# Layer-norm scaling moved from ScalarE to VectorE, and transposes moved behind attention

## The chip, the cores and the metric

The kernel runs on all 8 NeuronCores of one Trainium2 chip. Each core works on 4 of the 32 sequences and the cores don't talk to each other. The metric is the device time of the slowest core, in microseconds (us).

## The reference

For x of 32 sequences x 2048 tokens x 1024, the layer computes

```python
xn = _layernorm(x, axis=-1)
x = x + attn(xn, w_in, w_out) + ffn(xn, weight_q, weight_scale, bias)
```

Here attn is sliding-window attention with 16 heads of 64 and blocks of 512 tokens: each block of queries sees its own block of keys and the one before, masked to a window of 512, with a bias per head that grows with distance, a softmax and an output projection. The ffn quantises xn per token to 8 bits (scale = max|xn|/127, rounded), multiplies by an int8 weight matrix and scales back.

## The kernel before

A tile is one block of 512 tokens; a core has 16 of them, four per sequence. The first block of a sequence (n=0: tiles 0, 4, 8, 12) has 4 chunks of keys per head, the others (n>0) have 8. The program is written out by hand: each engine gets its list of instructions in the order in which the Python code emits them, and semaphores alone tie the engines together. The order of emission is the order of execution on each engine, and the DMAs of SP's queue stand in one such list too.

`emit_pre(t)` loads x of a tile into `x_tm` and computes its statistics on DVE (VectorE): bn_stats, bn_aggr, a maximum and a minimum over each token, and then a chain of small instructions for 1/sqrt(var) and the scales. The last of them is L351, and L354 is an empty instruction that raises the semaphore V. `emit_xnq_compute(t)` writes xn = x*rstd + bias in bf16 into `xn4`, with four ACT (ScalarE) instructions of 128x1024 (L366). `emit_xnq_transpose(t)` quantises x on DVE (`xq_chain`: two instructions into PSUM, L387 and L391, and two roundings, L396 and L400, for each of the four groups of 128 tokens), transposes xn and xq on PE (TensorE) by multiplying with the identity (L418), and copies the results from PSUM with ACT (L426). `emit_qkv(t)` computes q, k (L461, copies L472) and v (L484, copies L493), with the weights of q and k streamed by SP.

`emit_attn(t)` goes through 8 groups of two heads. For each chunk of keys PE computes scores (L632), ACT takes the exponential into one of 8 slots of `pe_buf` (L653, cut into slices of 64 to 512 columns by head), DVE multiplies a 128x128 part by a triangular mask (L666), and PE multiplies by V (L610), three chunks behind the scores. The two output banks of a group are normalised during the next group: ACT takes log and exp of the sum (L534, L538), PE spreads it over 64 partitions (L552, "ones"), ACT copies it (L557), and DVE multiplies (L563 into `o_fm`, L571 into `o_stage`, which a DMA brings to the upper half of `o_fm`). `emit_proj(t)` then does the output projection (L705) and the ffn's matmul (L717), and DVE adds up bias, x and both results (L729 to L744) and SP stores them.

PSUM has 8 banks, handed out in turn by `Banks`. In attention two of them hold outputs and six circulate.

In the main loop the statistics of tile t+1 and its L366 stand ahead of the attention of tile t on DVE and ACT; the quantising and the transposes of tile t+1 are called from a hook after group 4 of the attention of tile t.

Of the kernel before, what the change touches and what calls it, by code (L numbers as in the profile page):

```python
# [11 lines left out]
ALU = mybir.AluOpType  # L12
AF = mybir.ActivationFunctionType
# [128 lines left out]
def build_nc(n_seq=4, n_blk=4, taps=None):  # L142
    taps = taps or {}
    nc = bass.Bass("TRN2", target_bir_lowering=False)
    NT = n_seq * n_blk
# [19 lines left out]
    with ExitStack() as ctx:  # L165
# [13 lines left out]
        xn4 = sb("xn4", [128, 4096], BF16)  # L179
# [14 lines left out]
        stt = sb("stt", [128, 64], F32)  # L194
# [3 lines left out]
        C_MV, C_XMAX, C_XMIN, C_VEPS, C_SQ, C_R0, C_RTMP, C_RSTD = 0, 8, 12, 16, 20, 24, 28, 32  # L198
        C_BIASA, C_MX, C_AMAX, C_AM2, C_INV, C_ALPHA, C_BETA = 36, 40, 44, 48, 52, 56, 60
# [5 lines left out]
        P = Prog(sem_names)  # L205
# [7 lines left out]
        for dst, src in [(wsb_sb[:, :], wsbh), (biasb_sb[:, :], biasbh), (ident_sb[:, :], identh),  # L213
# [4 lines left out]
                  waits=[("LG", lg0)])  # L218
        lg0 = dma("gpsimd", wq_sb[:, :], wqh.rearrange("p a b -> p (a b)"), "LG",
                  waits=[("LG", lg0)])  # L220
# [15 lines left out]
        xn4_free = []  # L236
# [7 lines left out]
        zb_free = [[], []]  # L244
        zln_free = [[], []]
        prevT = 0
        stt_S_readers = 0
        TS = {}

        def tapit(name, src_ap, waits, engq="sync"):  # L250
            if name in tap_out:
                dma(engq, tap_out[name], src_ap, "TP",
                    waits=list(waits) + [("TP", P.cnt["TP"])])

        def tgeom(t):
            s_i, n_i = divmod(t, n_blk)
            return s_i, n_i, t % 2, n_i % 2, (n_i - 1) % 2, (s_i * n_blk + n_i) * TOK

        def emit_pre(t):
            s_i, n_i, par, slot, pslot, rowbase = tgeom(t)  # L260
            XS = "X%d" % par
            ld_x = dma("sync", x_tm[par][:, :].rearrange("p (a e) -> p a e", a=4),
                       xh[rowbase:rowbase + 512, :].rearrange("(a p) e -> p a e", p=128),
                       XS, waits=[x_free[par]])
            P.drain("vector")
            for tc in range(4):
                xs_ap = x_tm[par][:, 1024 * tc:1024 * (tc + 1)]
                P.op("vector", lambda e, a=xs_ap, tc=tc: e.bn_stats(  # L268
                    out=stbn[:, 12 * tc:12 * tc + 6], in_=a[:, 0:512]),
                    waits=[(XS, ld_x), ("S", stt_S_readers)])  # L270
                P.op("vector", lambda e, a=xs_ap, tc=tc: e.bn_stats(
                    out=stbn[:, 12 * tc + 6:12 * tc + 12], in_=a[:, 512:1024]))
            P.drain("vector")
            for tc in range(4):
                P.op("vector", lambda e, tc=tc: e.bn_aggr(
                    out=stt[:, C_MV + 2 * tc:C_MV + 2 * tc + 2], in_=stbn[:, 12 * tc:12 * (tc + 1)]))
# [15 lines left out]
                scalar=1, op=ALU.arith_shift_right))  # L292
# [59 lines left out]
                out=stt[:, C_BETA:C_BETA + 4], in0=mv_mean, scalar=-1.0,  # L352
                in1=stt[:, C_ALPHA:C_ALPHA + 4], op0=ALU.mult, op1=ALU.mult))
            v_stats = P.op("vector", lambda e: e.engine_nop(), inc="V")  # L354
            TS[t] = {"ldx": ld_x, "XS": XS, "vstats": v_stats}
            tapit("stats", stt[:, :], [("V", v_stats)])

        def emit_xnq_compute(t):
            nonlocal stt_S_readers
            s_i, n_i, par, slot, pslot, rowbase = tgeom(t)  # L360
            v_stats = TS[t]["vstats"]
            toks = []
            s_xn_last = 0
            for tc in range(4):
                xs_ap = x_tm[par][:, 1024 * tc:1024 * (tc + 1)]
                s_xn = P.op("scalar", lambda e, tc=tc, a=xs_ap: e.activation(  # L366
                    out=xn4[:, 1024 * tc:1024 * (tc + 1)], in_=a, func=AF.Identity,
                    bias=stt[:, C_BIASA + tc:C_BIASA + tc + 1], scale=stt[:, C_RSTD + tc:C_RSTD + tc + 1]),
                    waits=[("V", v_stats)] + xn4_free, inc="S")
                s_xn_last = s_xn  # L370
                toks.append(s_xn)
            TS[t]["xnqtok"] = toks
            stt_S_readers = s_xn_last

        def emit_xnq_transpose(t):
            nonlocal xn4_free
            s_i, n_i, par, slot, pslot, rowbase = tgeom(t)
            v_stats = TS[t]["vstats"]
            toks = TS[t]["xnqtok"]
            vq_toks = {}  # L380

            def xq_chain(tc):
                tcp = tc % 2
                xs_ap = x_tm[par][:, 1024 * tc:1024 * (tc + 1)]
                qb, qbw = banks.acquire()
                qb2, qbw2 = banks.acquire()
                P.op("vector", lambda e, tc=tc, a=xs_ap, qb=qb: e.tensor_scalar(  # L387
                    out=psum[qb][:, :], in0=a[:, 0:512], scalar1=stt[:, C_ALPHA + tc:C_ALPHA + tc + 1],
                    scalar2=stt[:, C_BETA + tc:C_BETA + tc + 1], op0=ALU.mult, op1=ALU.add),
                    waits=[("V", v_stats)] + qbw, inc="V")  # L390
                P.op("vector", lambda e, tc=tc, a=xs_ap, qb2=qb2: e.tensor_scalar(  # L391
                    out=psum[qb2][:, :], in0=a[:, 512:1024], scalar1=stt[:, C_ALPHA + tc:C_ALPHA + tc + 1],
                    scalar2=stt[:, C_BETA + tc:C_BETA + tc + 1], op0=ALU.mult, op1=ALU.add),
                    waits=qbw2, inc="V")
                P.drain("vector")
                v_q2 = P.op("vector", lambda e, o=xq2[tcp], qb=qb: e.tensor_scalar(  # L396
                    out=o[:, 0:512], in0=psum[qb][:, :], scalar1=MAGIC, scalar2=MAGIC,
                    op0=ALU.add, op1=ALU.subtract), waits=xq2_free[tcp], inc="V")
                banks.release(qb, [("V", v_q2)])
                v_q2 = P.op("vector", lambda e, o=xq2[tcp], qb2=qb2: e.tensor_scalar(  # L400
                    out=o[:, 512:1024], in0=psum[qb2][:, :], scalar1=MAGIC, scalar2=MAGIC,
                    op0=ALU.add, op1=ALU.subtract), inc="V")
                banks.release(qb2, [("V", v_q2)])
                vq_toks[tc] = v_q2

            def do_transpose(tc, half):
                tcp = tc % 2
                if half == 0:
                    wgate = [("S", toks[tc])]
                    lsrc, loff, dst_fm = xn4, 1024 * tc, xn_fm  # L410
                else:
                    wgate = [("V", vq_toks[tc])]
                    lsrc, loff, dst_fm = xq2[tcp], 0, xq_fm[par]
                for g in range(2):
                    b, bw = banks.acquire()
                    for j in range(4):
                        ec = g * 4 + j
                        tk = P.op("tensor", lambda e, b=b, j=j, ec=ec, lsrc=lsrc, loff=loff: e.matmul(  # L418
                            out=psum[b][:, 128 * j:128 * (j + 1)],
                            lhsT=lsrc[:, loff + 128 * ec:loff + 128 * (ec + 1)],  # L420
                            rhs=ident_sb[:, :], start=True, stop=True),
                            waits=(wgate + bw + [("SW", startup_LD), ("T", prevT)]) if j == 0 else (),
                            inc="T")
                    dst = dst_fm[:, :].rearrange("p (a b) -> p a b", b=512)[
                        :, g * 4:g * 4 + 4, 128 * tc:128 * (tc + 1)]
                    se = P.op("scalar", lambda e, b=b, d=dst: e.copy(  # L426
                        out=d, in_=psum[b][:, :].rearrange("p (a b) -> p a b", a=4)),
                        waits=[("T", tk), ("T", prevT)], inc="S")
                    banks.release(b, [("S", se)])
                if half == 1:  # L430
                    xq2_free[tcp] = [("T", P.cnt["T"])]

            xq_chain(0)
            xq_chain(1)
            for tc in range(4):
                do_transpose(tc, 0)
            do_transpose(0, 1)
            xq_chain(2)
            do_transpose(1, 1)
            xq_chain(3)  # L440
            do_transpose(2, 1)
            do_transpose(3, 1)
            xn4_free = [("T", P.cnt["T"])]
            TS[t]["sfm"] = ("S", P.cnt["S"])
            tapit("xn_fm", xn_fm[:, :], [TS[t]["sfm"]])
            tapit("xq_fm", xq_fm[par][:, :], [TS[t]["sfm"]])
# [309 lines left out]
            x_free[par] = ("V", P.cnt["V"])  # L756

        emit_pre(0)
        emit_xnq_compute(0)
        emit_xnq_transpose(0)  # L760
        emit_qkv(0)
        for t in range(NT):
            if t + 1 < NT:
                emit_pre(t + 1)
                emit_xnq_compute(t + 1)
                emit_attn(t, hooks={4: (lambda tt=t + 1: emit_xnq_transpose(tt))})
            else:
                emit_attn(t)
            emit_proj(t)
            prevT = P.cnt["T"]  # L770
            if t + 1 < NT:
                emit_qkv(t + 1)
            TS.pop(t - 1, None)
# [47 lines left out]
```

How the kernel before makes its waits and increments, by code:

```python
            def body(eng, ops_list=ops_list):  # L114
                hw = {}
                for fn, waits, inc, amt in ops_list:
                    for (s, v) in waits:
                        if v > hw.get(s, 0):
                            eng.wait_ge(sems[s], v)
                            hw[s] = v
                    inst = fn(eng)
                    if inc is not None:
                        inst.then_inc(sems[inc], amt)
```

## Time and profile before

| what | us |
|---|---|
| median of 2 runs | 3755.76 (3744.94 to 3766.57) |
| the profiled execution's own time | 3659.17 |
| its span on the slowest core, core 2 | 3657.6 |
| PE busy | 2519.1 |
| ACT busy | 1756.5 |
| DVE busy | 1372.7 |

The span runs from the first to the last instruction of the program on that core. Durations and places below are from the profiled execution. Busy time of PE includes matmuls at both levels of its clock. In the rows, times of the timeline are from the start of the span.

### The profile page before, as it was taken

The numbers are of one execution on the slowest core, as the hardware profiler recorded it, in microseconds if no ns is written. First come the engines' busy times: TensorE is split into PE (matmuls) and PEld (weight loads), VectorE is DVE, ScalarE is ACT, GpSimd is POOL, SyncE is SP. The second block draws the span as 40 slices with busy tenths as digits, with TensorE's granted clock in tenths as the row PEclk, the third lists the DMA queues.
The fourth block names the chain that finished last, engine by engine and source line by source line (L and its number), as shares of the span: only waits on it lengthen the run. The fifth ranks groups of instructions, "written<-read, shape, count | busy, mean of one in ns | idle before, by whom it ended". The sixth has DMA issues, their size and how long they took to land.

```text
span 3657.6 us, 41824 instructions; the slowest of 8 cores (3623.7 to 3657.6 us)
## 1 busy us (share of the span) xinstructions
PE 2519.1 (69%) x10560; PEld 1044.6 (29%) x10560; DVE 1372.7 (38%) x3552; ACT 1756.5 (48%) x4033; POOL 4.4 (0%) x10
## 2 busy tenths in 40 slices
PE   0467676776766767678676767768677576766777
PEld 0122232332322323233232323323233222322333
DVE  0343343433433344343442524345243433433314
ACT  0262652836626174471744437265382535618364
POOL 0000000000000000000000000000000000000000
PEclk9968668576585957759568685866858677595776
DMA  7302002011020201102002020200202111020100
GB/s 152 104 13 63 34 16 82 4 57 39 11 87 7 92 4 41 56 5 93 4 33 65 25 72 5 70 27 21 75 4 63 35 52 45 8 89 4 49 26 28
DMA packets 79523, 161.02 MB, mean 44 GB/s; under 512 B 8770, under 2 KB 17218, under 8 KB 78914
## 3 DMA queue, kind: packets, MB, share of 16 engines
q1 hardware_dynamic: 76786, 147.85, 12.4%
q0 software_dynamic: 2512, 10.49, 1.6%
q8 instruction: 102, 1.67, 0.2%
q14 instruction: 123, 1.01, 0.1%
HBM read 119.51 MB, written 37.75 MB: 43 GB/s over the span
## 4 chain that ended last, share of the span: by engine, by line
PE 41%; DMA 16%; ACT 14%; DVE 12%; issue 8%; ACTq 6%; DVEq 3%; SPq 0%; POOLq 0%
PE ps L610 12%; ACT pe_buf L653 9%; DMA wqk<-w2bf 9%; PE ps L461 8%; PE ps L632 6%; PE ps L705 6%; PE ps L717 5%; ACTq L105 5%; DMA x_tm<-x 4%; PE ps L552 3%; DVEq L105 3%; ACT zln L534 2%; DVE stt L277 2%; PE ps L418 2%; DVE stt L279 1%
## 5 line engine op out<-in xcount | busy, mean ns | idle before, releaser
L653 ACT ACTIVATE pe_buf<-ps,ebias_sb 128x128 bf16<-128x128 f32 (+4 forms) x2560 | 904.2, 527 | 160.6 <-PE ps L632 157.8
L632 PE MATMUL ps<-q_fm,k_st 64*128 64x512 bf16 (+3 forms) x1792 | 510.0, 424 | 505.6 <-ACT pe_buf L653 492.1
L666 DVE TENSOR_TENSOR pe_buf<-pe_buf,tripo_sb 128x128 bf16<-128x128 bf16 x1792 | 391.2, 223 | 1065.1 <-ACT pe_buf L653 1013.5
L461 PE MATMUL ps<-xn_fm,wqk 128*128 128x512 bf16 x2048 | 516.3, 404 | 277.3 <-DMA wqk<-w2bf 266.3
L610 PE MATMUL ps<-pe_buf,v_st 128*65 128x128 bf16 (+3 forms) x2368 | 608.2, 405 | 15.0 <-ACT pe_buf L653 10.9
L472 ACT CAST q_fm<-ps 128x512 bf16<-128x512 f32 x128 | 75.0, 586 | 846.9 <-PE ps L461 846.9
L610 PEld LDWEIGHTS ps<-pe_buf,v_st 128*65 128x65 bf16 x2368 | 292.4, 157 | 336.5 <-issue 260.0
L632 PEld LDWEIGHTS ps<-q_fm,k_st 64*128 64x128 bf16 x1792 | 130.1, 102 | 864.0 <-issue 851.1
L461 PEld LDWEIGHTS ps<-xn_fm,wqk 128*128 128x128 bf16 x2048 | 196.5, 102 | 596.9 <-issue 430.9
L268 DVE BATCH_NORM_STATS2 stbn<-x_tm 128x6 f32<-128x512 f32 x64 | 43.6, 681 | 842.3 <-DMA x_tm<-x 842.3
L705 PE MATMUL ps<-wout_sb,o_fm 128*128 128x512 bf16 x1024 | 263.0, 412 | 10.0 <-DMA o_fm<-o_stage 10.0
L717 PE MATMUL ps<-wq_sb,xq_fm 128*128 128x512 bf16 x1024 | 231.8, 379 | 0.0
L484 PE MATMUL ps<-wv_sb,xn_fm 128*128 128x512 bf16 x1024 | 223.6, 379 | 0.0
L552 PE MATMUL ps<-zr_sb,ones_sb 1*64 1x512 bf16 x256 | 140.6, 615 | 103.3 <-ACT zr_sb L538 103.3
L472 ACT CAST k_st<-ps 128x512 bf16<-128x512 f32 x128 | 75.0, 586 | 251.3 <-PE ps L461 251.3
L418 PE MATMUL ps<-ident_sb,xn 128*128 128x128 bf16 x512 | 63.9, 295 | 171.4 <-ACT xn L366 129.7
L538 ACT ACTIVATE zr_sb<-zln 1x512 bf16<-1x512 f32 x256 | 160.8, 628 | 21.5 <-issue 1.1
L534 ACT ACTIVATE zln<-ps 1x512 f32<-1x512 f32 x256 | 148.9, 582 | 22.9 <-PE ps L610 20.1
L557 ACT CAST zb_sb<-ps 64x512 bf16<-64x512 f32 x256 | 137.3, 578 | 46.1 <-PE ps L552 41.0
L705 PEld LDWEIGHTS ps<-wout_sb,o_fm 128*128 128x128 bf16 x1024 | 103.4, 103 | 160.5 <-issue 59.8
L729 DVE SCALAR_TENSOR_TENSOR ffn<-ps,xs_sb,wsb_sb 128x512 f32<-128x512 f32 x128 | 95.5, 746 | 138.0 <-PE ps L717 138.0
L493 ACT CAST v_st<-ps 128x512 bf16<-128x512 f32 x128 | 75.3, 588 | 145.7 <-PE ps L484 145.7
(50 smaller groups left out, 1506.9 us busy)
## 6 DMA issues: line engine op xcount, KB each, us to landing
wqk<-w2bf SPq DMA_DIRECT2D x256, 256.0 KB, 2.6
x_tm<-x SPq DMA_DIRECT2D x16, 2048.0 KB, 8.3
out<-outhf SPq DMA_DIRECT2D x128, 256.0 KB, 2.0
o_fm<-o_stage SPq DMA_DIRECT2D x128, 64.0 KB, 1.9
k_st<-w POOLq DMA_DIRECT2D x2, 2048.0 KB, 16.1
w2bf<-k_st SPq DMA_DIRECT2D x2, 2048.0 KB
wv_sb<-wv POOLq DMA_DIRECT2D x1, 2048.0 KB, 18.7
wout_sb<-wout POOLq DMA_DIRECT2D x1, 2048.0 KB, 18.0
```

The source lines that it names most:

```text
L105: self.ops[eng].append((lambda e: e.drain(), [], None, 1))
L461: tk = P.op("tensor", lambda e, b=b, ec=ec, fp=fp: e.matmul(out=psum[b][:, :], lhsT=wqk_buf[fp][:, 128 * ec:128 * (ec + 1)], rhs=xn_fm[:, ...
L484: tk = P.op("tensor", lambda e, b=b, ec=ec, tc=tc, half=half: e.matmul(out=psum[b][:, :], lhsT=xn_fm[:, 512 * ec + 128 * tc:512 * ec + 128 ...
L534: P.op("scalar", lambda e, ob=ob, sl=sl: e.activation(out=zln2[0:1, 512 * sl:512 * (sl + 1)], in_=psum[ob][64:65, :], func=AF.Ln), waits=[ ...
L538: vz = P.op("scalar", lambda e, sl=sl: e.activation(out=zr_sb[0:1, 512 * sl:512 * (sl + 1)], in_=zln2[0:1, 512 * sl:512 * (sl + 1)], func= ...
L552: tzb = P.op("tensor", lambda e, zbk=zbk, sl=sl: e.matmul(out=psum[zbk][0:64, :], lhsT=ones_sb[0:1, :], rhs=zr_sb[0:1, 512 * sl:512 * (sl ...
L610: slp=slp, first=pv_first[hh], lastp=lastp: e.matmul(out=psum[ob][0:65, c0:c0 + cw], lhsT=vsl, rhs=pe_buf[:, 512 * slp + (c0 - qsp):512 * ...
L632: qs=qs, w=w, ksl=ksl: e.matmul(out=psum[b][:, 0:w], lhsT=ksl, rhs=q_fm[base2:base2 + 64, pr2 * 512 + qs:pr2 * 512 + qs + w], start=True, ...
L653: sl_pe=sl_pe, ecol=ecol: e.activation(out=pe_buf[:, 512 * sl_pe + a0 - qs:512 * sl_pe + a1 - qs], in_=psum[b][:, a0 - qs:a1 - qs], func=A ...
L666: gm = P.op("vector", lambda e, sl_pe=sl_pe, tloc=tloc, tsel=tsel: e.tensor_tensor(out=pe_buf[:, 512 * sl_pe + tloc:512 * sl_pe + tloc + 128],
L705: tk = P.op("tensor", lambda e, b=b, pr=pr, tc=tc, half=half: e.matmul(out=psum[b][:, :], lhsT=o_fm[:, pr * 512 + 128 * tc:pr * 512 + 128 ...
L717: tk = P.op("tensor", lambda e, b=b, ec=ec, tc=tc, half=half, par=par: e.matmul(out=psum[b][:, :], lhsT=xq_fm[par][:, 512 * ec + 128 * tc: ...
```

## The change

Two things are done. The four L366 instructions leave ACT and become four DVE tensor_scalar instructions at the end of `emit_pre`, behind L354; the wait of the first statistics instruction on ACT's readers of `stt` goes, since there are none left. And the hook goes: quantising and transposes of tile t+1 are emitted after the whole attention of tile t, ahead of `emit_proj(t)`.

```diff
@@ emit_pre
-                    waits=[(XS, ld_x), ("S", stt_S_readers)])
+                    waits=[(XS, ld_x)])
...
             v_stats = P.op("vector", lambda e: e.engine_nop(), inc="V")
-            TS[t] = {"ldx": ld_x, "XS": XS, "vstats": v_stats}
...
-        def emit_xnq_compute(t):
...
             for tc in range(4):
                 xs_ap = x_tm[par][:, 1024 * tc:1024 * (tc + 1)]
-                s_xn = P.op("scalar", lambda e, tc=tc, a=xs_ap: e.activation(
-                    out=xn4[:, 1024 * tc:1024 * (tc + 1)], in_=a, func=AF.Identity,
-                    bias=stt[:, C_BIASA + tc:C_BIASA + tc + 1], scale=stt[:, C_RSTD + tc:C_RSTD + tc + 1]),
-                    waits=[("V", v_stats)] + xn4_free, inc="S")
+                v_xn = P.op("vector", lambda e, tc=tc, a=xs_ap: e.tensor_scalar(
+                    out=xn4[:, 1024 * tc:1024 * (tc + 1)], in0=a,
+                    scalar1=stt[:, C_RSTD + tc:C_RSTD + tc + 1],
+                    scalar2=stt[:, C_BIASA + tc:C_BIASA + tc + 1],
+                    op0=ALU.mult, op1=ALU.add),
+                    waits=[("V", v_stats)] + xn4_free, inc="V")
@@ emit_xnq_transpose
-                    wgate = [("S", toks[tc])]
+                    wgate = [toks[tc]]
@@ main loop
         emit_pre(0)
-        emit_xnq_compute(0)
         emit_xnq_transpose(0)
         emit_qkv(0)
         for t in range(NT):
             if t + 1 < NT:
                 emit_pre(t + 1)
-                emit_xnq_compute(t + 1)
-                emit_attn(t, hooks={4: (lambda tt=t + 1: emit_xnq_transpose(tt))})
-            else:
-                emit_attn(t)
+            emit_attn(t)
+            if t + 1 < NT:
+                emit_xnq_transpose(t + 1)
             emit_proj(t)
```

Lines behind the edit move: L387, L418, L610, L632, L653, L666 and L705 of before are L379, L410, L602, L624, L645, L658 and L697 of after.

On PE, before, in tile 0 around the hook: the last P·V of group 4 (L610), the transposes, and the scores of group 5 (L632).

```order
L632 MATMUL ps<-q_fm,k_st 128x128 x2
L610 MATMUL ps<-pe_buf,v_st 65x512 x2
L610 MATMUL ps<-pe_buf,v_st 65x384 x2
L610 MATMUL ps<-pe_buf,v_st 65x256 x2
L610 MATMUL ps<-pe_buf,v_st 65x128 x2
L418 MATMUL ps<-ident_sb,xn 128x128 x32
L418 MATMUL ps<-ident_sb,xq_0 128x128 x8
L418 MATMUL ps<-ident_sb,xq_1 128x128 x8
L418 MATMUL ps<-ident_sb,xq_0 128x128 x8
L418 MATMUL ps<-ident_sb,xq_1 128x128 x8
L632 MATMUL ps<-q_fm,k_st 128x512 x2
```

On PE, after, at the end of the attention of tile 0: the last P·V of group 7 (L602), the two ones matmuls (L544), the transposes (L410), and the projection (L697).

```order
L602 MATMUL ps<-pe_buf,v_st 65x128 x2
L544 MATMUL ps<-zr_sb,ones_sb 64x512 x2
L410 MATMUL ps<-ident_sb,xn 128x128 x32
L410 MATMUL ps<-ident_sb,xq_0 128x128 x8
L410 MATMUL ps<-ident_sb,xq_1 128x128 x8
L410 MATMUL ps<-ident_sb,xq_0 128x128 x8
L410 MATMUL ps<-ident_sb,xq_1 128x128 x8
L697 MATMUL ps<-wout_sb,o_fm 128x512 x16
```

The 64 transposes have moved from between two groups of attention to between attention and projection; in the middle L602 is now followed by L624 at once.

On DVE, before, at the start of the attention of tile 0: the end of the statistics and the masks of groups 0 and 1 (L666), which are followed by the first output multiplies.

```order
L344 TENSOR_TENSOR stt<-stt 128x4
L348 TENSOR_SCALAR stt<-stt 128x4
L351 SCALAR_TENSOR_TENSOR stt<-stt 128x4
L354 ISA
L666 TENSOR_TENSOR pe_buf<-pe_buf,tripo_sb 128x128 x14
L563 TENSOR_TENSOR o_fm<-ps,zb_sb 64x512
```

On DVE, after, at the same place.

```order
L343 TENSOR_TENSOR stt<-stt 128x4
L347 TENSOR_SCALAR stt<-stt 128x4
L350 SCALAR_TENSOR_TENSOR stt<-stt 128x4
L353 ISA
L357 TENSOR_SCALAR xn<-x_tm,stt 128x1024 x4
L658 TENSOR_TENSOR pe_buf<-pe_buf,tripo_sb 128x128 x14
```

Four instructions of 1024 columns now stand between the statistics and the first mask. On ACT the four of the same size that stood between the last copy of v (L493) and the first exponential (L653) are gone, and nothing has come in their place.

## Rows read from the trace of the kernel before

**Rows 1.** The page, the chain that ended last: share of the span by engine

```profile
PE 41%; DMA 16%; ACT 14%; DVE 12%; issue 8%; ACTq 6%; DVEq 3%; SPq 0%; POOLq 0%
```

**Rows 2.** Timelines of ACT and PE, tile 1: start, duration, what [idle before]

```profile
399.29 4.63 ACT L366 ACTIVATE xn<-x_tm,stt 128x1024 bf16<-128x1024 f32 x4 [9.39 <-DVEq L354]
403.83 13.45 ACT L653 ACTIVATE pe_buf<-ps,ebias_sb 128x64 bf16<-128x64 f32 x60
...
404.46 0.83 PE L632 MATMUL ps<-q_fm,k_st 64*128 64x512 bf16 x2 [14.10 <-ACT pe_buf L653]
```

**Rows 3.** Timeline of all engines at the start of tile 4's attention

```profile
1093.00 4.63 ACT L366 ACTIVATE xn<-x_tm,stt 128x1024 bf16<-128x1024 f32 x4 [9.23 <-DVEq L354]
1097.54 3.42 ACT L653 ACTIVATE pe_buf<-ps,ebias_sb 128x512 bf16<-128x512 f32 x8
...
1099.18 2.66 PE L610 MATMUL ps<-pe_buf,v_st 128*65 128x512 bf16 x8
...
1101.77 0.93 PE L632 MATMUL ps<-q_fm,k_st 64*128 64x512 bf16 x4
```

**Rows 4.** Timelines of DVE and PE around the hook of tile 4

```profile
1137.01 0.80 DVE L387 TENSOR_SCALAR ps<-x_tm,stt 128x512 f32<-128x512 f32 x1
1137.73 0.80 DVE L391 TENSOR_SCALAR ps<-x_tm,stt 128x512 f32<-128x512 f32 x1
...
1143.64 0.81 DVE L387 TENSOR_SCALAR ps<-x_tm,stt 128x512 f32<-128x512 f32 x1 [0.92 <-ACT xn_fm L426]
...
1148.22 0.69 DVE L396 TENSOR_SCALAR xq<-ps 128x512 bf16<-128x512 f32 x1 [0.16 <-issue]
1148.83 0.68 DVE L400 TENSOR_SCALAR xq<-ps 128x512 bf16<-128x512 f32 x1
...
1137.56 0.86 PE L418 MATMUL ps<-ident_sb,xn 128*128 128x128 bf16 x8
...
1149.76 1.01 PE L418 MATMUL ps<-ident_sb,xq 128*128 128x128 bf16 x8 [1.98 <-DVE xq L400]
1150.71 1.91 PE L632 MATMUL ps<-q_fm,k_st 64*128 64x512 bf16 x5
```

**Rows 5.** Timelines: projection's start in tile 1; first exponential and projection's start, tile 15

```profile
526.20 3.17 PE L705 MATMUL ps<-wout_sb,o_fm 128*128 128x512 bf16 x7
...
3511.05 13.49 ACT L653 ACTIVATE pe_buf<-ps,ebias_sb 128x64 bf16<-128x64 f32 x60
...
3620.00 3.17 PE L705 MATMUL ps<-wout_sb,o_fm 128*128 128x512 bf16 x7
```

**Rows 6.** Timelines of PE and DVE at the end of tile 4's attention

```profile
1180.82 3.17 PE L705 MATMUL ps<-wout_sb,o_fm 128*128 128x512 bf16 x7
...
1181.79 0.68 DVE L571 TENSOR_TENSOR o_stage<-ps,zb_sb 64x512 bf16<-64x512 f32 x1 [0.25 <-ACT zb_sb L557]
```

**Rows 7.** Waits: who waited for whom, us in total, times, longest

```profile
PE ps L705 <- DMA o_fm<-o_stage: 10.0, 16, 0.9
```

**Rows 8.** Groups by line and form: count, busy us, mean ns, idle before

```profile
L666 DVE TENSOR_TENSOR pe_buf<-pe_buf,tripo_sb 128x128 bf16<-128x128 bf16 x1792 | 391.2, 223 | 1065.1 <-ACT pe_buf L653 1013.5
L735 DVE TENSOR_TENSOR ffn<-ffn,biasb_sb 128x512 f32<-128x512 f32 x128 | 88.6, 693 | 11.8
L279 DVE TENSOR_REDUCE stt<-x_tm 128x1 f32<-128x1024 f32 x64 | 77.4, 1210 | 0.0
L366 ACT ACTIVATE xn<-x_tm,stt 128x1024 bf16<-128x1024 f32 x64 | 74.1, 1229 | 142.1 <-DVEq L354 142.1
L387 DVE TENSOR_SCALAR ps<-x_tm,stt 128x512 f32<-128x512 f32 x64 | 51.6, 806 | 15.6 <-ACT xn_fm L426 15.4
```

**Rows 9.** Windows, start of tile 4's projection: busy by engine, then PE's granted clock, DMA

```profile
1184.90:1189.30 4.40, 4.40 (x11) 1.59 (x12) 0.00 (x0) 0.00 (x0) 0.00 (x0) 0.50 0.00 0
1189.30:1213.30 24.00, 24.00 (x111) 10.68 (x109) 18.11 (x26) 0.00 (x0) 0.00 (x0) 1.00 0.17 66
```

**Rows 10.** Timeline of DVE in the prologue: third quantising chain

```profile
134.11 0.81 DVE L387 TENSOR_SCALAR ps<-x_tm,stt 128x512 f32<-128x512 f32 x1 [1.72 <-ACT xn_fm L426]
```

More of the change, by code:

```diff
@@ L246, in build_nc @@
         prevT = 0
-        stt_S_readers = 0
         TS = {}
@@ L354, in emit_pre @@
             v_stats = P.op("vector", lambda e: e.engine_nop(), inc="V")
-            TS[t] = {"ldx": ld_x, "XS": XS, "vstats": v_stats}
-            tapit("stats", stt[:, :], [("V", v_stats)])
-        def emit_xnq_compute(t):
-            nonlocal stt_S_readers
-            s_i, n_i, par, slot, pslot, rowbase = tgeom(t)
-            v_stats = TS[t]["vstats"]
             toks = []
-            s_xn_last = 0
             for tc in range(4):
                 xs_ap = x_tm[par][:, 1024 * tc:1024 * (tc + 1)]
-                s_xn = P.op("scalar", lambda e, tc=tc, a=xs_ap: e.activation(
-                    out=xn4[:, 1024 * tc:1024 * (tc + 1)], in_=a, func=AF.Identity,
-                    bias=stt[:, C_BIASA + tc:C_BIASA + tc + 1], scale=stt[:, C_RSTD + tc:C_RSTD + tc + 1]),
-                    waits=[("V", v_stats)] + xn4_free, inc="S")
[L370 to L373, printed above, removed]
+                v_xn = P.op("vector", lambda e, tc=tc, a=xs_ap: e.tensor_scalar(
[4 more added lines that the diff above has]
+                    waits=[("V", v_stats)] + xn4_free, inc="V")
+                toks.append(("V", v_xn))
+            TS[t] = {"ldx": ld_x, "XS": XS, "vstats": v_stats, "xnqtok": toks}
+            tapit("stats", stt[:, :], [("V", v_stats)])
         def emit_xnq_transpose(t):
```

## The prediction

> **What bounds the kernel now.** I read the page's head and chain first. The chain that ended last spends 41% in PE, 16% in DMA, 14% in ACT and 12% in DVE [rows 1]: no engine bounds the whole, the stages of a tile follow each other, and each has to be read by itself. So I went to the timeline, engine by engine, at the three places that the change touches in each of the 15 tiles with a successor.
>
> First, the start of attention. In tile 1 ACT stands idle 9.39 us until the statistics of the next tile are done on DVE at about 399.3 us, then normalises for 4.63 us, and only at 403.83 does the first exponential run; PE has sat idle 14.10 us [rows 2]. The first mask multiply, and with it the first P·V, is later still. Tile 4, a first block with half the chunks, shows the same: normalising from 1093.00, exponentials from 1097.54, P·V from 1099.18, group 1's scores from 1101.77 [rows 3].
>
> Second, the place after group 4. PE leaves attention at 1137.56 for the transposes and is back at scores at 1150.71: 13.15 us. They are paced by DVE, whose quantising runs from 1137.01 to about 1149.5 [rows 4]. Nothing of attention lies beside it, as the stretch from first exponential to projection shows: 403.83 to 526.20 (122.37 us) in tile 1, which has the transposes, and 3511.05 to 3620.00 (108.95 us) in tile 15, which has not: 13.4 us [rows 2, 5].
>
> Third, the seam between attention and projection: PE's first projection matmul is at 1180.82 in tile 4, while DVE still has the last o_stage multiply to do, to 1182.46 [rows 6], and PE later waits for the o_fm DMA, 10.0 us over 16 tiles, 0.63 us each [rows 7].
>
> **Part 1: normalising goes from ACT to DVE.** Of ACT, 64 instructions of 1229 ns go [rows 8]; 64 tensor_scalar of 128x1024 come on DVE, between the statistics and the masks. The trace has no such instruction. Its nearest row is L387: same operation, same source, the same two per-partition scalars, half as wide and into PSUM, 806 ns, 0.72 us from start to start [rows 4, 8]. Below: the pace of the rounding L396 to L400, also 512 wide, 1148.22 to 1148.83, 0.61 us each [rows 4], 2.4 us in all. Above: twice L387's pace, 1.44 us each, 5.8 us in all. Which end is nearer depends on whether DVE takes more than one f32 element per step when one source and the target lie in SBUF. The 1024-wide reductions take 1210 ns, the 512-wide adds 693 ns, about 1.0 ns per element; down that line a 128-wide operation would cost 300 ns, but the bf16 mask multiply takes 223 [rows 8]. So a faster pace exists in this trace, though not shown for f32. I take L387's own pace for the double width, 0.72 us each, 2.9 us in all.
>
> The Trainium skill bears on this: "VectorE: DVE Perf Modes", on the perf-mode tiers, says that an f32 tensor_scalar with source and target in SBUF runs two elements per cycle, and a reduction never more than one. No row here shows the first; the reductions agree with the second. By its formula (half of 1024 plus 151 cycles at 0.96 GHz) one would take an estimated 0.69 us and four 2.8 us, which leaves the sum where it is.
>
> What it does to the start of attention, n>0 (11 tiles: 1 to 3, 5 to 7, 9 to 11, 13, 14). ACT no longer waits for DVE, so it does the exponentials of the first four chunks during the statistics. They are half of group 0's 60 exponentials: 13.45/2 = 6.7 us [rows 2], and there are 9.4 us of idle time for them. They stop there: pe_buf has 8 slots, and P·V needs the masks, which now stand behind statistics and normalising on DVE. Masks start at 399.3+2.9 = 402.2; the first P·V 0.3 later; two P·V, the next scores (0.42 us each, 0.83 for two [rows 2]) and the step to ACT, an estimate of 1.0 more: the second half starts at 403.5. Before, it started at 403.83+6.7 = 410.5. Gain 7.0 us a tile, 77 us in all (with the ends of DVE's price: 7.5 and 4.1 a tile).
>
> n=0 (4 tiles: 0, 4, 8, 12). Group 0 has 8 P·V and group 1's scores come behind all of them. Masks from 1093.0+2.9 = 1095.9, P·V from 1096.2, 2.66 us long [rows 3], group 1's scores at 1098.9 instead of 1101.77: 2.9 us a tile, 11.6 in all. Here early exponentials help little, since before they ran just ahead of the P·V anyway.
>
> **Part 2: the transposes go behind attention.** Removed: 13.2 us a tile, between the two measures above. Added: DVE comes free for quantising only at 1182.46. Its work took 12.5 us in the middle, 0.92 of it a wait for a bank that ACT had not emptied [rows 4]; behind attention no output bank is held, so I take 11.5. Then 0.25 to PE and 0.95 for the last eight transposes (1149.76 to 1150.71): projection starts at about 1195.1 instead of 1180.8, 14.3 us later. The wait for the o_fm DMA, 0.63, is covered by then: 13.7 net. The move costs 0.5 us a tile, 7.5 in all. SP's queue is passed by nothing: the x load still stands ahead of attention, the o_fm copies and out stores keep their order. If the cover for the first P·V (ACT's head start) were gone, only this loss would stay.
>
> PE's clock: in tile 4 PE was granted 0.50 up to 1189.3, 8.5 us after the projection's first matmul, and 1.00 from there [rows 6, 9], the lower and upper of its levels (1.2 and 2.4 GHz). The transposes now ahead of it keep PE no busier than the end of attention did, so I leave this alone, with 0.5 us a tile either way.
>
> Prologue: DVE normalises before it quantises, +2.9 us, but a 1.72 us wait of its third chain for a bank [rows 10] goes: +1.3.
>
> **Sum.** 77+11.6-7.5-1.3 = 80 us less than the profiled execution's 3659.17 (span 3657.6): 3579. The runs shown have a median of 3755.76, 97 us above it; I take the same 80 us off: **3676 us**, 2.1% less. About 2% is also what a measurement of this kernel tells from no change.
>
> **Rivals.**
> *DVE takes one f32 element at a time.* For it: the 1210 ns reductions. Against: the 223 ns mask. Four at 1.21 us are 4.8, so 1.9 us more in each of 15 tiles: 29 us back, gain 51, 3705 us.
>
> *The head start is worth nothing*, because something else than ACT (banks, pe_buf, PE's order) holds group 0: only the 9 us of loss stay, 3765 us. For it: at 1083 to 1098 PE stands idle with its scores done, and DVE is late in either version. Against: in tile 15, which has no statistics, the 60 exponentials run in one piece of 13.49 us [rows 5], so in group 0 ACT is the bound, and half of its work is moved out.
>
> *Slower: projection stays at the low clock.* Transposes in bursts with DVE's pace between them now stand right ahead of the 128 projection matmuls. At the low level one takes 3.17/7 = 0.45 us [rows 6], at the high one 24.0/111 = 0.22 [rows 9]. It decides from 25 more matmuls at the low level a tile on (80/15 = 5.3 us). If half of the 128 ran low, 44 more than the 20 of tile 4, that is 44 x 0.21 = 9.3 us a tile, 139 in all: 3815 us. For it: 8.5 us of projection, 4.40 of them without a gap, passed at 0.50 before the clock rose. Against: the clock rose in the midst of projection then, and PE's stream there is unbroken. "TensorE: Matmul & The Clock Gate", Part 1, in the Trainium skill says that the throttled state is the default and sustained activity releases it; by that rule the stream of projection itself raises the clock, which rows 9 agree with, and this rival falls.
>
> **How the numbers follow.** Forecast 0.66, one element at a time 0.20, no head start 0.06, low clock 0.08. The forecast's own bounds are 3659 to 3700 (DVE price, clock, seam). The 2% line lies at 3681, 5 us off it, so three quarters of the forecast's chance counts as faster by over 2% (0.50); the rest of it, the second and the third rival are within 2% (0.42); the low clock is slower (0.08). Range 3615 to 3740: up past the second case, short of the slower ones; down by half of the 97 us by which the runs stand above the profiled execution, since I can't say whether they will again.
>
> **What would show it.** Right: ACT's 128x64 exponentials start within 1 us of the last v_st cast; DVE's new row has a mean near 0.8 us; tile 1's second half of group 0 starts 4.3 us after the statistics; group 4 to 5 has no pause; projection starts some 14 us after the last ones matmul. Wrong: a mean of 1.2 to 1.4 us in that row, ACT idle in the second half of group 0, more than 16 us at the seam, or 0.50 in the clock column beyond the first 8 us of projection.

## The result, and the profile after

The changed kernel takes 3557.39 us (median of 11 runs, 3554.5 to 3592.97), the kernel before 3668.52 us (median of 10). The ratio is 0.9713, with a 95% interval of 0.9692 to 0.9734: 2.9% faster, some 105 us. The forecast was 80 us less, and 3676 us. The two runs of before from which the 3676 was worked out, 3744.94 and 3766.57, lie above all eight later ones, 3657 to 3680. In some executions the cores of one die are granted a lower clock and the time is longer (3746.79 us in one later run of the kernel before, at 0.67 against 0.72 on the other die); the ratios leave these out, and the first two runs look like two of them, though their clocks are not on record. So there are two misses to explain: the level from which I subtracted, and 25 us of gain.

The page of the kernel after, slowest core:

```profile
span 3569.9 us, 41819 instructions; the slowest of 8 cores (3530.7 to 3569.9 us)
...
PE 2503.1 (70%) x10560; PEld 1045.1 (29%) x10560; DVE 1407.6 (39%) x3616; ACT 1691.4 (47%) x3969; POOL 4.4 (0%) x10
...
PE 46%; DMA 14%; DVE 13%; ACT 11%; issue 7%; ACTq 6%; DVEq 3%; SPq 0%; POOLq 0%
```

In the chain that ended last PE has gone from 41% to 46% and ACT from 14% to 11% [rows 1]: less of the span hangs on ACT.

The start of attention, timelines of ACT and then DVE in tile 2 of the slowest core ([rows 2] show tile 1 of before):

```profile
624.10 6.83 ACT L645 ACTIVATE pe_buf<-ps,ebias_sb 128x64 bf16<-128x64 f32 x30
637.50 6.82 ACT L645 ACTIVATE pe_buf<-ps,ebias_sb 128x64 bf16<-128x64 f32 x30 [6.56 <-PE ps L624]
...
632.90 0.16 DVE L350 SCALAR_TENSOR_TENSOR stt<-stt 128x4 f32<-128x4 f32 x1
633.18 2.98 DVE L357 TENSOR_SCALAR xn<-x_tm,stt 128x1024 bf16<-128x1024 f32 x4
636.07 1.17 DVE L658 TENSOR_TENSOR pe_buf<-pe_buf,tripo_sb 128x128 bf16<-128x128 bf16 x8
```

Where ACT had one piece of 60 exponentials, it has two of 30. The first starts within 0.5 us of the last copy of v and is done 2.1 us before the statistics. Then ACT waits 6.56 us, and the second begins at 637.50, 4.4 us after the statistics (forecast 4.3). On this core the 11 tiles with n>0 and a successor all have these two halves, with 3.3 to 8.0 us between them. Eight masks stand ready and follow each other at once.

The seam, the place between attention and projection, timelines of PE and DVE in tile 4 (before: [rows 6]):

```profile
1153.60 0.60 PE L544 MATMUL ps<-zr_sb,ones_sb 1*64 1x512 bf16 x1 [0.59 <-ACT zr_sb L530]
1154.31 2.20 PE L410 MATMUL ps<-ident_sb,xn 128*128 128x128 bf16 x16
...
1167.43 0.86 PE L410 MATMUL ps<-ident_sb,xq 128*128 128x128 bf16 x8 [2.17 <-DVE xq L392]
1168.09 5.09 PE L697 MATMUL ps<-wout_sb,o_fm 128*128 128x512 bf16 x16
...
1155.70 0.80 DVE L379 TENSOR_SCALAR ps<-x_tm,stt 128x512 f32<-128x512 f32 x1
...
1166.61 0.68 DVE L392 TENSOR_SCALAR xq<-ps 128x512 bf16<-128x512 f32 x1
```

DVE quantises from 1155.70 to 1167.29, 11.6 us (forecast 11.5), and the 16 projection matmuls run in one piece, without the wait of [rows 7]. From the start of the last ones matmul to the projection it is 14.5 us; before, with ones at 1180.29 and projection at 1180.82, it was 0.5 us.

The new instruction, from the groups; then the waits of after, and the same ones of before:

```profile
L357 DVE TENSOR_SCALAR xn<-x_tm,stt 128x1024 bf16<-128x1024 f32 x64 | 47.7, 809 | 1.9 <-DVEq L353 0.2
```

```profile
PE ps L624 <- ACT pe_buf L645: 261.7, 263, 2.7
...
PE ps L602 <- DVE pe_buf L658: 163.2, 26, 12.5
...
PE ps L697 <- DMA o_fm<-o_stage: 0.6, 1, 0.6
```

```profile
PE ps L632 <- ACT pe_buf L653: 492.1, 314, 15.3
...
PE ps L610 <- DVE pe_buf L666: 3.3, 12, 0.3
```

809 ns is the duration of L387, the row of half the width from which I took it [rows 8]. The waits show what is now late. PE waits 230 us less for ACT to take the scores out of their banks, and 160 us more for the masks ahead of P·V, which stand behind statistics and normalising on DVE.

To see where time went in each kernel I divided tiles 0 to 14 of all eight cores at five points of PE's timeline: the start of the first score, the start of the first projection matmul, the end of the last one (the ffn's are counted in), the start of the first matmul with new weights, and the start of the first one of v. The gap is the time between projection and weights. Means in us:

| kernel | first score to projection, n=0 / n>0 | projection | gap | weights' stage | mean span |
|---|---|---|---|---|---|
| before | 98.4 / 137.0 | 30.4 | 8.3 | 40.7 | 3641 |
| after | 95.6 / 130.5 | 29.6 | 8.2 | 40.6 | 3552 |
| p1_dve_only | 95.1 / 130.2 | 30.5 | 8.3 | 40.6 | 3555 |
| p2_move_only | 99.2 / 137.6 | 29.6 | 8.3 | 40.2 | 3629 |
| p2_again | 99.1 / 137.5 | 29.4 | 8.3 | 40.2 | 3625 |
| xn_twice | 99.0 / 133.8 | 29.5 | 8.3 | 40.3 | 3593 |
| spread | 89.9 / 125.8 | 29.4 | 8.2 | 40.4 | 3467 |
| spread2 | 86.1 / 122.2 | 29.2 | 8.3 | 40.6 | 3410 |
| ffn_first | 98.0 / 136.5 | 30.2 | 5.8 | 40.9 | 3598 |
| gapfill | 98.2 / 137.0 | 30.5 | 8.3 | 38.7 | 3611 |
| prefill | 98.2 / 136.7 | 30.8 | 8.3 | 40.6 | 3641 |
| best | 86.0 / 122.2 | 29.8 | 6.0 | 38.7 | 3358 |
| before, cores 4 to 7 | 98.2 / 136.9 | 30.4 | 8.3 | 40.8 | 3641 |
| after, cores 4 to 7 | 95.5 / 130.5 | 29.4 | 8.2 | 40.6 | 3546 |
| ffn_first, cores 4 to 7 | 98.1 / 136.8 | 29.9 | 5.8 | 40.8 | 3593 |
| best, cores 0 to 3 | 86.0 / 122.4 | 29.4 | 5.9 | 38.5 | 3347 |

In the profiled executions of after, ffn_first and best the four cores of one die had stretches at a clock of 0.81; the last rows have the cores that had none. The mean span of after is 89 us less than that of before and not 105. On its cores 4 to 7 it is 95 us less.

### The profile page after: what moved, and what is told of

It is laid out like the page before. It is cut to its first block, busy times and chain, and to the rows that moved or that the text cites. A ratio compares the mean times of both kernels' runs of the same rounds, so it can differ in the third digit from the quotient of the medians.

```text
span 3569.9 us, 41819 instructions; the slowest of 8 cores (3530.7 to 3569.9 us)
## 1 busy us (share of the span) xinstructions
PE 2503.1 (70%) x10560; PEld 1045.1 (29%) x10560; DVE 1407.6 (39%) x3616; ACT 1691.4 (47%) x3969; POOL 4.4 (0%) x10
## 4 chain that ended last, share of the span: by engine, by line
PE 46%; DMA 14%; DVE 13%; ACT 11%; issue 7%; ACTq 6%; DVEq 3%; SPq 0%; POOLq 0%
PE ps L602 13%; PE ps L453 9%; DMA wqk<-w2bf 8%; PE ps L697 7%; PE ps L624 7%; ACT pe_buf L645 7%; ACTq L105 6%; PE ps L709 5%; DMA x_tm<-x 4%; PE ps L544 3%; DVEq L105 3%; ACT zln L526 2%; DVE stt L276 2%; DVE stt L278 1%; PE ps L410 1%
## 5 line engine op out<-in xcount | busy, mean ns | idle before, releaser
L645 ACT ACTIVATE pe_buf<-ps,ebias_sb 128x128 bf16<-128x128 f32 (+4 forms) x2560 | 908.1, 502 | 294.6 <-PE ps L624 291.8
L658 DVE TENSOR_TENSOR pe_buf<-pe_buf,tripo_sb 128x128 bf16<-128x128 bf16 x1792 | 381.7, 223 | 928.1 <-ACT pe_buf L645 876.8
L602 PE MATMUL ps<-pe_buf,v_st 128*65 128x128 bf16 (+3 forms) x2368 | 601.8, 403 | 179.5 <-DVE pe_buf L658 163.2
L624 PE MATMUL ps<-q_fm,k_st 64*128 64x512 bf16 (+3 forms) x1792 | 484.3, 422 | 271.5 <-ACT pe_buf L645 261.7
L602 PEld LDWEIGHTS ps<-pe_buf,v_st 128*65 128x65 bf16 x2368 | 294.5, 157 | 491.6 <-issue 415.5
L624 PEld LDWEIGHTS ps<-q_fm,k_st 64*128 64x128 bf16 x1792 | 122.6, 101 | 610.3 <-issue 594.9
L697 PE MATMUL ps<-wout_sb,o_fm 128*128 128x512 bf16 x1024 | 262.4, 415 | 0.6 <-DMA o_fm<-o_stage 0.6
L544 PE MATMUL ps<-zr_sb,ones_sb 1*64 1x512 bf16 x256 | 140.8, 616 | 103.4 <-ACT zr_sb L530 103.4
L410 PE MATMUL ps<-ident_sb,xn 128*128 128x128 bf16 x512 | 70.9, 302 | 188.1 <-DVE xn L357 131.5
L721 DVE SCALAR_TENSOR_TENSOR ffn<-ps,xs_sb,wsb_sb 128x512 f32<-128x512 f32 x128 | 95.5, 746 | 168.4 <-PE ps L709 168.4
L526 ACT ACTIVATE zln<-ps 1x512 f32<-1x512 f32 x256 | 149.1, 583 | 22.9 <-PE ps L602 20.2
L549 ACT CAST zb_sb<-ps 64x512 bf16<-64x512 f32 x256 | 137.4, 580 | 45.4 <-PE ps L544 40.2
L697 PEld LDWEIGHTS ps<-wout_sb,o_fm 128*128 128x128 bf16 x1024 | 107.7, 106 | 141.5 <-issue 46.2
```

What stands on the lines that cost most here:

```text
L526: P.op("scalar", lambda e, ob=ob, sl=sl: e.activation(out=zln2[0:1, 512 * sl:512 * (sl + 1)], in_=psum[ob][64:65, :], func=AF.Ln), waits=[ ...
L544: tzb = P.op("tensor", lambda e, zbk=zbk, sl=sl: e.matmul(out=psum[zbk][0:64, :], lhsT=ones_sb[0:1, :], rhs=zr_sb[0:1, 512 * sl:512 * (sl ...
L602: slp=slp, first=pv_first[hh], lastp=lastp: e.matmul(out=psum[ob][0:65, c0:c0 + cw], lhsT=vsl, rhs=pe_buf[:, 512 * slp + (c0 - qsp):512 * ...
L624: qs=qs, w=w, ksl=ksl: e.matmul(out=psum[b][:, 0:w], lhsT=ksl, rhs=q_fm[base2:base2 + 64, pr2 * 512 + qs:pr2 * 512 + qs + w], start=True, ...
L645: sl_pe=sl_pe, ecol=ecol: e.activation(out=pe_buf[:, 512 * sl_pe + a0 - qs:512 * sl_pe + a1 - qs], in_=psum[b][:, a0 - qs:a1 - qs], func=A ...
L658: gm = P.op("vector", lambda e, sl_pe=sl_pe, tloc=tloc, tsel=tsel: e.tensor_tensor(out=pe_buf[:, 512 * sl_pe + tloc:512 * sl_pe + tloc + 128],
```

## The experiments

**p1_dve_only and p2_move_only** take the change apart. The first is the kernel after with the hook back in its place:

```diff
-            emit_attn(t)
-            if t + 1 < NT:
-                emit_xnq_transpose(t + 1)
+                emit_attn(t, hooks={4: (lambda tt=t + 1: emit_xnq_transpose(tt))})
+            else:
+                emit_attn(t)
             emit_proj(t)
```

> Only the first half of the change: DVE normalises ahead of the masks, the transposes stay behind group 4. My theory (the head start of ACT is what pays): 7.0 us in each of 11 tiles with n>0 and 2.9 us in each of 4 with n=0, 88 us less than before, ratio 0.976; from first scores to projection 7 us less in tile 2 and 3 us less in tile 4. Rival (what the whole gained beyond my 80 us, some 25 us, came from moving the transposes, because the start of projection is better placed there): this run stays at 0.976 and the move alone is clearly faster than before. Second rival (the 25 us lie in the first half): this run is at 0.970 or below.

Measured: 3572.96 us, ratio 0.9773 (0.9729 to 0.9818), 83 us less by the ratio and 88 by the medians. The attention stage is 3.3 us shorter with n=0 and 6.8 with n>0; I had 2.9 and 7.0. The head start is worth what was forecast. The interval (67 to 99 us) leaves room for a few us more, but the stages of the trace show no surplus of 25 us here.

The second is the kernel before with the opposite edit, ACT still normalising.

> Only the second half: ACT still normalises, the transposes go behind attention. My theory: 14.3 us more at the seam, 13.2 us less in the middle, 0.6 us of DMA wait covered: 0.5 us a tile more, 7 us in all, ratio 1.002. Rival (the unexplained 25 us are here): 18 to 25 us less than before, ratio 0.994, with the projection itself shorter than the 30.4 us that it takes before.

Measured: 3648.6 us, ratio 0.9969 (0.9938 to 1.0). **p2_again**, the same kernel in more rounds:

> The move alone a second time, in more rounds, since its first run (0.9969) lay between my 1.002 and no gain. Its trace against that of before: attention up to the projection 0.7 us longer a tile, projection 0.85 us shorter, so 0.2 us less a tile, 2 to 3 us in all. If that is all, the ratio is 0.999; if the 12 us of the first run are the move's own, it is 0.9965 again, and the rest must show in one stage of both traces alike, the weights' stage (L461) being the one to look at (40.7 us before, 40.2 in the first run of the move).

Measured: 3647.51 us in 14 runs, ratio 0.9966 (0.9946 to 0.9986). The two agree: the move by itself gains 12 us (5 to 20 by the second interval), where I had a loss of 7.5. By the table it costs 0.8 and 0.5 to 0.7 us a tile in the attention stage, not 1.1; it gains 0.8 to 1.0 in the projection, not 0.6; and the weights' stage, of which I expected nothing, is 0.5 us shorter in both runs. That is 0.8 us a tile, 12 us in 15 tiles.

**xn_twice** doubles the cost that came on DVE:

```diff
-            for tc in range(4):
+            first = {}
+            for tc in [0, 1, 2, 3, 0, 1, 2, 3]:
...
-                    waits=[("V", v_stats)] + xn4_free, inc="V")
+                    waits=[("V", first.get(tc, v_stats))] + xn4_free, inc="V")
+                first[tc] = v_xn
                 toks.append(("V", v_xn))
+            toks = toks[4:]
```

> The changed kernel with the four normalising instructions issued a second time on DVE, same values into the same place. My theory (masks wait for DVE in every tile, so its time there is on the path one to one): 2.9 us more in each of 15 tiles and in the prologue, 46 us more than the changed kernel, ratio to before 0.984. Rival (something else than DVE ends the start of attention): no more than 10 us more, ratio 0.974 or below.

Measured: 3608.43 us, ratio 0.9854 (0.9832 to 0.9876); 51 us above the kernel after. The attention stage grew by 3.3 to 3.4 us a tile. ACT in its tile 2:

```profile
620.84 6.80 ACT L648 ACTIVATE pe_buf<-ps,ebias_sb 128x64 bf16<-128x64 f32 x30
637.67 6.80 ACT L648 ACTIVATE pe_buf<-ps,ebias_sb 128x64 bf16<-128x64 f32 x30 [10.04 <-PE ps L627]
```

The idle time between the two halves went from 6.56 to 10.04 us. DVE's block ahead of the masks lies on the path at least one to one: 2.9 us more of it made the stage 3.3 to 3.4 us longer. Where the last 0.4 us come from was not looked into.

**spread** takes that block away. `emit_pre` becomes a generator, and attention calls one of its pieces behind each chunk:

```diff
+                    if pieces is not None and (pr_grp > 0 or ci > 0):
+                        next(pieces, None)
                     if ci == 1:
                         flush_div_a(2)
...
-                emit_pre(t + 1)
-            emit_attn(t)
+                pieces = pre_pieces(t + 1)
+                next(pieces)
+            emit_attn(t, pieces=pieces)
```

> The changed kernel with the statistics and the normalising of the next tile cut into 23 pieces, one behind each chunk of the present tile's attention, so that no block of DVE work stands ahead of the first masks. My theory: group 0 then runs as in tile 15; against the changed kernel 6.9 us less in 11 tiles and 11.3 us less in 4, 120 us in all, less some 20 us by which pieces delay masks: ratio to before 0.945. Rival (in attention DVE's pieces hold the masks and through them PE, since PE is the busiest): half of that or less, ratio 0.957 or above.

Measured: 3484.92 us, ratio 0.9517 (0.9495 to 0.9538). Of the 6.9 us for n>0 4.7 came (130.5 to 125.8), of the 11.3 for n=0 5.7. What ate the rest is in PE's timeline of tile 4:

```profile
1068.97 0.53 PE L614 MATMUL ps<-pe_buf,v_st 128*65 128x128 bf16 x2 [0.56 <-DVE pe_buf L670]
...
1078.64 0.52 PE L614 MATMUL ps<-pe_buf,v_st 128*65 128x128 bf16 x2 [0.47 <-DVE pe_buf L670]
```

and in DVE's just ahead of it:

```profile
1066.18 1.21 DVE L281 TENSOR_REDUCE stt<-x_tm 128x1 f32<-128x1024 f32 x1
1067.31 0.68 DVE L567 TENSOR_TENSOR o_fm<-ps,zb_sb 64x512 bf16<-64x512 f32 x1
1067.91 0.67 DVE L575 TENSOR_TENSOR o_stage<-ps,zb_sb 64x512 bf16<-64x512 f32 x1
1068.51 0.34 DVE L670 TENSOR_TENSOR pe_buf<-pe_buf,tripo_sb 128x128 bf16<-128x128 bf16 x2
```

A piece of 1.2 us in the chunk in which the two output multiplies stand too makes the group's last masks late, and PE waits 0.5 us for them.

**spread2** leaves that chunk free, and places two of the four quantising chains inside attention where n>0:

```diff
-                    if pieces is not None and (pr_grp > 0 or ci > 0):
+                    if pieces is not None and (pr_grp > 0 or ci > 0) and ci != len(chunks) - 2:
...
+                if pieces is not None and n_i > 0 and pr_grp in (5, 6):
+                    xq_chain(t + 1, pr_grp - 5)
```

> The spread kernel, with no piece in the chunk in which the output multiplies stand, pieces in group 0 from its second chunk as before, and for tiles with n>0 the first two quantising chains placed after groups 5 and 6 instead of behind attention. My theory: in tiles with n=0 attention up to projection falls from 89.9 by about 3 us; with n>0 the seam is 5.6 us of DVE shorter, of which PE's transposes of xn give back 2 and the masks 1, so 2.5 us a tile: 39 us less than spread, ratio to before 0.941. Rival (the chains hold two of the six banks and the masks in groups 5 and 6, and cost there what they save behind): ratio 0.949 or above.

Measured: 3432.72 us, ratio 0.9379 (0.9354 to 0.9403). The attention stage fell by 3.8 us with n=0 and 3.6 with n>0, more than the 3 and 2.5 expected. With n=0 only the first of the two edits acts, so the late masks account for 3.8 of the 5.6 us that spread had missed there; with n>0 the two edits were not tried apart. Group 0 is again one piece, as in tile 15 [rows 5]:

```profile
593.41 13.49 ACT L662 ACTIVATE pe_buf<-ps,ebias_sb 128x64 bf16<-128x64 f32 x60
```

**ffn_first** is the kernel before with the two matmul loops of `emit_proj` exchanged: the ffn's (now L705) come ahead of the output projection's (now L717). It was meant to isolate the wait for the o_fm DMA.

> The kernel before with the ffn's 16 matmuls put ahead of the output projection's 16 in each quarter of the tile, nothing else. It isolates the wait for the o_fm DMA, 0.63 us a tile, that the move covers. My theory: the wait goes, 10 us in 16 tiles, ratio 0.997, and the projection stage takes 29.7 us instead of 30.4. Rival (the shorter projection after the move comes from the clock, not from the wait): the stage stays within 0.2 us of 30.4 and the ratio at 1.000.

Measured: 3614.92 us, ratio 0.9882 (0.9848 to 0.9916), 43 us less, four times what I expected, and mostly for another reason.

The wait is gone. In the mean of all cores the projection shortened by only 0.2 us, as the rival had it, but cores 0 to 3 of this execution had some 210 us each at 0.81. On cores 4 to 7 it went from 30.4 to 29.9 us, 0.5 less, which is the theory's side (0.6 to 0.7). It is less than the 0.8 us of gap that went: in the kernel before, each tile has 8.1 projection matmuls that start 0.38 to 0.50 us apart and 0.8 us of gap; in ffn_first 10.6 such matmuls and no gap. The clock rises at the same point either way, 4.4 us in. So what fills the gap are matmuls at the low level that would have run at the high one a little later, and part of the 0.8 us is lost again: an estimate from these rows is 0.8 less 2.5 x 0.21, 0.3 us, and 0.5 was measured.

Most of the 43 us comes from the gap ahead of the weights, 8.3 to 5.8 us, 38 us in 15 tiles. The waits, of ffn_first and then of before:

```profile
PE ps L461 <- DMA wqk<-w2bf: 225.2, 153, 6.3
...
DVE outhf L744 <- PE ps L717: 76.7, 64, 2.5
```

```profile
PE ps L461 <- DMA wqk<-w2bf: 266.3, 143, 9.0
...
DVE ffn L729 <- PE ps L717: 138.0, 64, 8.5
```

Three of DVE's four instructions per half need only the ffn's result. With that result first, they run beside the output projection. DVE ends 2.2 us behind PE's last matmul instead of 4.7 (mean of all tiles), and the last out store is issued as much sooner, and with it the first weights, which stand behind it on SP's queue.

**gapfill** asks whether the weights' stage follows the clock. Into the kernel before, between projection and weights, go 30 matmuls whose result nobody reads:

```diff
             if t + 1 < NT:
+                fill(30)
                 emit_qkv(t + 1)
```

where `fill(n)` takes a bank and multiplies `ident_sb` by 512 columns of `wout_sb` n times.

> The kernel before, with 30 matmuls of 512 columns without use put on PE between a tile's projection and the next tile's weights' stage, where PE sits idle 8.3 us a tile for the first weights; at the high clock they take 6.5 us. With them the clock should not fall, so the 4.8 us at the low clock at the start of that stage (mean of all cores) go. Theory (the stage's length follows the clock, so the 0.5 us that the moved transposes gained there are the clock's): the stage falls from 40.7 us by 1.5 to 2.4, ratio 0.992. Rival (the stage is paced by the weights' DMA, and the 0.5 us have another cause): it stays within 0.3 us of 40.7, ratio 1.000.

Measured: 3643.91 us, ratio 0.996 (0.993 to 0.9989). The stage fell from 40.7 to 38.7 us, and its time at the low clock, by the records of the granted clock, from 4.8 to 1.0 us. That is 0.53 us for each us at the low clock. The fill and the stage behind it in tile 4, windows of gapfill (the last three columns are granted clock, DMA share and GB/s):

```profile
1207.00:1215.00 8.00, 7.19 (x34) 3.04 (x32) 4.81 (x7) 0.00 (x0) 0.00 (x0) 1.00 0.30 101
1215.00:1254.00 39.00, 28.43 (x124) 11.24 (x125) 0.00 (x0) 8.79 (x15) 0.00 (x0) 1.00 0.40 116
```

The clock is 1.00 throughout. The theory holds in the trace, where the mean span is 30 us less; the timed runs show 15 us (4 to 26), so the sign and half of the size, and what makes the difference is open.

**prefill** puts 3 such matmuls behind the last P·V of a tile in the kernel before:

```diff
             flush_div_a(len(divq))
+            fill(3)
             flush_div_b(len(divq2))
```

> The kernel before, with 3 matmuls of 512 columns without use on PE after the last P·V of a tile, in the 1.4 us for which PE waits for the last normalisation. Theory (the clock rises sooner when the time just ahead of the projection holds more matmuls, as with the moved transposes): the time at the low clock in the projection falls from 4.4 us towards 3.5, the projection from 30.4 towards 30.0, ratio 0.998. Rival (1.3 us more of work there is too little, or the wait for the o_fm DMA decides): low time within 0.2 us of 4.4, ratio 1.000 or above.

Measured: 3668.45 us, ratio 1.0052 (1.0017 to 1.0087): slightly slower, while the mean span of the profiled execution is the same, 3641. The low time in the projection fell from 4.4 to 3.4 us as the theory has it, but the projection grew from 30.4 to 30.8 us. PE's timeline in tile 4 of the slowest core, and its waits:

```profile
1178.76 3.12 PE L715 MATMUL ps<-wout_sb,o_fm 128*128 128x512 bf16 x7
1183.15 2.10 PE L715 MATMUL ps<-wout_sb,o_fm 128*128 128x512 bf16 x9 [1.26 <-DMA o_fm<-o_stage]
```

```profile
PE ps L715 <- DMA o_fm<-o_stage: 22.9, 16, 2.1
```

The sooner the clock rises, the longer PE waits at the eighth matmul: the landing of o_fm sets its time (6.8 us behind the last P·V, 6.9 in before), and 10.0 us of wait became 22.9. That explains why nothing is gained. What is lost has another cause, which the records of the granted clock show. In 33 of the 120 tiles the clock was high at the first projection matmul, fell to the low level within the projection and rose again; before has none of these. Tile 4 of core 0 is one, with the fall behind a wait of 2.48 us:

```profile
1174.50:1179.80 5.30, 2.81 (x14) 1.16 (x14) 1.36 (x2) 0.71 (x2) 0.00 (x0) 1.00 0.05 14
1179.90:1183.20 3.30, 3.30 (x9) 1.18 (x8) 0.00 (x0) 0.00 (x0) 0.00 (x0) 0.50 0.00 0
```

In these 33 the projection took 31.8 us. In the 59 in which the clock was not low behind the eighth matmul it took 30.0, as it did in the 38 such tiles of before. So a sooner rise buys nothing as long as that wait stands behind it, and can cost a second fall.

**best** puts spread2, the order of ffn_first and a `fill(24)` together.

> spread2 with the ffn's matmuls ahead of the output projection's, and 24 matmuls without use in the gap before the weights. If the parts add up: 0.938, less 0.012 for the order of the matmuls, less what gapfill gives (0 to 0.008): ratio 0.918 to 0.926. If the shorter tail of DVE is used up by the filling or by the transposes: 0.932 or above.

Measured: 3373.24 us, ratio to before 0.9222 (0.9185 to 0.9258), 5% below the changed kernel. The attention stage is as in spread2, the gap 6.0 us and the weights' stage 38.7, and the ratios add up too: 0.938 less 0.012 (ffn_first) less 0.004 (gapfill) is 0.922. How much each adds in this company was not tried apart.

## Why the prediction was right and wrong

**Right: what bounds the start of attention.** The steps of part 1 came out one by one: 809 ns for the new instruction, 0.72 us from start to start, the second half 4.4 us after the statistics, 6.8 us a tile with n>0 and 3.3 with n=0 in p1_dve_only. The rival "one f32 element at a time" falls with the 809 ns for 1024 columns, where the 1024-wide reductions take 1209. The Trainium skill ("VectorE: DVE Perf Modes", on the perf-mode tiers) says that an f32 tensor_scalar with source and target in SBUF runs two elements per cycle, and this trace agrees in kind. By that page's formula the estimate was 0.69 us; the measured 0.81 is 0.12 above it. L387's 806 ns is above the 693 of an add of the same width by as much, so that surplus may be the two per-partition scalars, which no run isolated. "The head start is worth nothing" falls with p1_dve_only and xn_twice.

**Wrong: the sum of part 2, a loss of 0.5 us a tile and 7.5 us in all.** Two terms of it were mis-sized and one was missing. What was added less what was removed came to some 0.6 us a tile and not 1.1: I took 13.2 us for the pause in the middle, near the lower of my two readings, where the comparison with tile 15 had given 13.4, and 14.3 for the seam, where before and after differ by 14.0 (14.5 less 0.5). For the projection I had only the covered DMA wait, at its 0.63 us of idle time, and the projection shortened by 0.8 to 1.0: ffn_first puts the wait alone at 0.5 us, and the rest goes with the clock, below. And the weights' stage, 0.5 us a tile, stood in no term. So the move gains 0.8 us a tile where I had a loss of 0.5, 12 us in all and 20 us from what I had. That is most of the 25 us.

**Wrong: leaving the clock alone.** I bounded it by half a us a tile and gave no term for the weights' stage. The 8.5 us at 0.50 that I read in tile 4 of one core is nearly twice the mean: the projections of before have 4.4 us at the low clock. The records of the granted clock give 3.4 to 3.7 us a tile at the low clock in the projection once the transposes stand ahead of it, against 4.4, and 4.2 in the weights' stage, against 4.8. gapfill shows that the latter stage pays 0.53 us per us of low clock, so 0.6 us less of it explain 0.3 of the 0.5 us. Why the clock falls a little later there was not settled, nor is the remainder; the kernel after itself has 40.6 us in this stage, and only the kernels with the move alone, xn_twice and spread lie clearly below before. The rival "projection stays at the low clock" had the sign wrong: with the transposes ahead of it the projection spends a little less time at the low level, not more.

**Wrong: the level.** Of the some 118 us between 3676 and the result, 93 are the level (3755.76 against the 3662 that ratio and result give for the kernel before) and 25 the gain. The profiled execution, 3659.17, was the better base than the median of two runs. I saw the 97 us between them, and took only half of them into the range, which therefore ended at 3615. Subtracted from the profiled execution, the forecast was 3579, 0.6% from the result; it rested on a part 2 with the wrong sign, so the nearness of that number is no proof of the sum.

**The prologue** was to cost 1.3 us. The first score came 2.2 us later in p1_dve_only and 5.1 in the kernel after (means of the cores). Of this 0.6 and 2.9 us are the landing of x, which differs between executions; behind it the prologue is 1.6 and 2.2 us longer.

What remains: 83 us (first half) and 12 us (move) make 95, and the whole was measured at 105 with an interval of 98 to 113. The intervals of the parts (67 to 99 and 5 to 20) cover the difference, and nothing shows that more is left to explain.

## What to carry to other kernels

An instruction that waits at the head of an in-order engine holds up all that is queued behind it; when it moves to another engine, count what can now run ahead of it and up to which buffer, and what has become late in its place. A block of work for the next tile belongs in pieces between the chunks of the present one, outside the chunks in which its engine already has something to deliver: with two of the quantising chains treated likewise (spread2), that was worth some 120 us, more than the change itself. Price a stage that is moved on both sides of the seam and in the stage behind it, and take the base of an absolute forecast from an execution whose trace you have, or make the range reach down to it.

## What the runs showed of the hardware

- Independent matmuls ahead of a stage that waits for DMAs change it: the weights' stage went from 40.7 to 38.7 us in gapfill when PE was kept at work in the 8 us before, though its matmuls wait for weights in either case.
- Idle time of PE while it is at the low clock costs less than its length: ffn_first removed 0.8 us of gap a tile, the clock rose at the same point, and the projection shortened by 0.5 us (cores 4 to 7).
- A clock that rises sooner can buy nothing: prefill took 1 us a tile from the low clock in the projection, but the wait for a DMA behind it grew by 0.8 us, in 33 of 120 tiles the clock fell again, and the projection grew by 0.4 us.
- A tensor_scalar on DVE with an f32 source and a bf16 target in SBUF and two per-partition scalars took 809 ns for 1024 columns; with an f32 target in PSUM it took 803 to 806 ns for 512.
- Beside 0.50 and 1.00 the granted clock was 0.81 in some stretches, in the 4 cores of one die and for 94 to 223 us a core, in the profiled executions of after, ffn_first and best alone of the twelve. A window of core 3 of after:

```profile
380.00:404.00 24.00, 22.95 (x90) 9.12 (x88) 14.40 (x21) 6.58 (x12) 0.00 (x0) 0.81 0.26 100
```
